# Routing of the first half cut into three pieces and moved behind the last groups, scatters moved behind all inverse roots

## The reference, cut to what matters

```
x = x + attn_a(layernorm(x))      # arccos kernel: 1 - arccos(s)/pi to the power 9, then a product
x = x + ffn(layernorm(x))         # mixture of experts, first time
x = x + attn_b(layernorm(x))      # linear attention: 16 heads of 8, elu feature map
x = x + ffn(layernorm(x))         # mixture of experts, second time

ffn(x):
    logits = x @ gate_w + gate_b
    top_w, top_i = top_k(logits, 2)               # 2 of 8 experts for each token
    gw = softmax(top_w)
    out = sum over the 2 chosen experts e of gw * (gelu(x @ w1[e] + b1[e]) @ w2[e] + b2[e])
    shared = gelu(x @ ws1 + bs1) @ ws2 + bs2
    return out + shared
```

## Time and profile before

| | us |
|---|---|
| median of 3 runs | 698.61 (694.57 to 699.79) |
| profiled execution, its own time | 695.24 |
| its span in the trace | 693.4 |
| busy in the span: DVE / PE / ACT / POOL | 552.1 / 497.8 / 465.5 / 375.5 |

### The profile page before, as it was taken

The page is one execution under the profiler, slowest core; times in us unless marked ns, Lnnn a source line. Parts: engine busy times, 40 slices in busy tenths (PEclk is TensorE's granted clock), DMA queues, the critical chain, the costliest instruction groups (busy, mean ns, idle before and its releaser), DMA issues.

```text
span 693.4 us, 14048 instructions
## 1 busy us (share of the span) xinstructions
PE 497.8 (72%) x3817; PEld 360.3 (52%) x3818; DVE 552.1 (80%) x1229; ACT 465.5 (67%) x937; POOL 375.5 (54%) x382
## 2 busy tenths in 40 slices
PE   1276725655456998999977678757569999999760
PEld 1132305555422446787866466646224469888650
DVE  4989666978668985899989778786679859998991
ACT  1379988998234665989966767845535569999750
POOL 5032201323477776677757722226677737777773
PEclk9999977968558999999999999967689999999996
DMA  8700000000011144444473310001111444545943
GB/s 277 215 8 0 1 0 0 1 1 0 16 47 47 52 115 81 91 98 100 104 194 85 96 35 1 1 9 36 39 48 57 115 80 94 100 101 137 228 112 125
DMA packets 95054, 51.12 MB, mean 74 GB/s; under 512 B 76026, under 2 KB 84180, under 8 KB 94996
## 3 DMA queue, kind: packets, MB, share of 16 engines
q1 hardware_dynamic: 85908, 31.67, 20.5%
q0 software_dynamic: 9088, 18.76, 9.0%
HBM read 16.27 MB, written 23.90 MB: 58 GB/s over the span
## 4 chain that ended last, share of the span: by engine, by line
PE 27%; DVE 21%; issue 17%; ACT 13%; POOL 11%; SPq 8%; DMA 3%; DVEq 0%; POOLq 0%; ACTq 0%
POOL routed_rows L724 8%; SPq L561 5%; PE PC L1107 5%; PE PC L1314 4%; DVE big L1901 2%; DMA RR<-expert_results 2%; DVE RR L1915 2%; ACT SC L834 2%; SPq L568 2%; ACT big L934 2%; PE PA L1125 2%; DVE big L1539 2%; PE PC L1316 2%; PE PA L1296 1%; PE PA L1298 1%
## 5 line engine op out<-in xcount | busy, mean ns | idle before, releaser
L778 POOL DMA_INDIRECT expert_results<-RR,DG x156 | 171.1, 1097 | 73.0 <-issue 45.9
L724 POOL DMA_INDIRECT routed_rows<-big,SLQ x128 | 137.5, 1074 | 56.1 <-issue 45.0
L1314 PE MATMUL PC<-W,big 128*128 x624 | 117.4, 275 | 25.9 <-DVE RR L1915 24.7
L1026 ACT ACTIVATE SC<-PA,B1T,scl 128x256 f32<-128x256 f32 x208 | 100.5, 571 | 21.6 <-PE PA L1298 12.2
L1904 DVE SCALAR_TENSOR_TENSOR big<-SC,scl,big 128x1024 f16<-128x1024 f32 x78 | 100.3, 1286 | 2.8
L1316 PE MATMUL PC<-W,big 128*128 x468 | 86.5, 221 | 0.0
L1314 PEld LDWEIGHTS PC<-W,big 128*128 128x128 f16 x624 | 57.9, 98 | 41.5 <-issue 36.8
L1107 PE MATMUL PC<-QW,big 128*128 128x128 f32 x256 | 42.7, 345 | 42.8 <-DVE big L1539 28.1
L1901 DVE TENSOR_SCALAR big<-SC,scl 128x1024 f16<-128x1024 f32 x78 | 65.1, 835 | 5.8 <-ACT SC L1026 5.8
L671 POOL TENSOR_TENSOR RS<-VA,halfneg 128x4 f32<-128x4 f32 x24 | 28.4, 1185 | 67.9 <-DVE VA L1573 67.8
L1107 PEld LDWEIGHTS PC<-QW,big 128*128 128x128 f32 x256 | 41.2, 257 | 45.0 <-DVE big L1539 29.4
(11 more groups left out here) (284 smaller groups left out, 1268.3 us busy)
## 6 DMA issues: line engine op xcount, KB each, us to landing
RR<-expert_results SPq DMA_DIRECT2D x16, 512.0 KB, 4.2
routed_rows<-pad_zeros SPq DMA_DIRECT2D x23, 128.0 KB
expert_results<-RR,DG POOLq DMA_INDIRECT x156
X<-n_L_attn_a_hidden_states SPq DMA_DIRECT2D x2, 1024.0 KB, 6.5
big<-in_L_ffn_w SPq DMA_DIRECT2D x1, 2048.0 KB, 9.0
routed_rows<-big,SLQ POOLq DMA_INDIRECT x128, 2.4
out_x<-X SPq DMA_DIRECT2D x8, 256.0 KB
big<-routed_rows SPq DMA_TRANSPOSE x78
```

The source lines that it names most:

```text
L724: pool.indirect_dma_start(routed, bass.IndirectOffsetOnAxis(ap=SLQ[:, slot, t, c:c + 1], axis=0), XHL[:, slot, t, c, :].bitcast(I32), None ...
L778: pool.indirect_dma_start(results, bass.IndirectOffsetOnAxis(ap=DG[:, k, r, 0:1], axis=0), YT[:, k, r, :], None).then_inc(result_stored[k] ...
L1026: ins = act.activation(HF[:, k % 3, b * RU:(b + 1) * RU], up_out(k, b), ACT.Gelu, scale=INV1, bias=B1T[:, bass.ds(b1_at + b, 1)])
L1314: last = pe.matmul(both, hh, W2[:, :, at], start=(b == 0), stop=(b == HB - 1))
```

## The change

Three things move; no arithmetic operation is added or taken away.

1. routing is cut into choose, place and gates. For the first half they stand behind the last groups' steps on DVE: in layer 0 choose(0) at the end of step 16, place(0) at the end of step 17, gates(0) and rows(0) behind the add of group 7, then rows(1) and rows(2) at the ends of steps 20 and 22; in layer 1 choose(0) at the end of step 8, place(0) behind the add of group 7 and ahead of its shift, gates(0) and rows(0) behind that shift, rows(1) and rows(2) behind the low part of group 7. rows(3) stands behind the routing of the second half. Places come before gates now.
2. PE's route(0) moves with it: behind the value product of group 7 in layer 0, behind the projection of group 7 in layer 1, there in bank A in place of bank C.
3. On POOL all inverse roots (and in layer 0 all x_scale) come ahead of the first scatter.

The core of the diff (renamed helpers and the unchanged steps are left out):

```diff
              (3, "gate"), (1, "turn_out"))
-LIN_RING = {"kv": "A", "out": "A", "turn_out": "A", "turn_x": "B", "state": "B", "gate_turn": "B",
+LIN_RING = {"kv": "A", "out": "A", "turn_out": "A", "route": "A", "turn_x": "B", "state": "B", "gate_turn": "B",
...
-                if (what, n - lag) == ("project", groups // 2 + 1):
+                t.take(what, n - lag, LIN_RING[what])
+                if (what, n - lag) == ("project", groups - 1):
                     for slot in range(2):
-                        t.take("route", slot, "C")
-                t.take(what, n - lag, LIN_RING[what])
+                        t.take("route", slot, LIN_RING["route"])
     return t.turn
...
             if layer:
-                USES.append(("linear", (3 * per, 3 * per), (3 * per, 3 * per), (3 * per + 1, 3 * per + 1)))
+                USES.append(("linear", (3 * per + 1, 3 * per + 1), (3 * per, 3 * per), (3 * per, 3 * per)))
...
             if half == 0:
-                return PC[slot], c_read[slot], lin_free("route", slot)
+                return PA[slot], a_read[slot], lin_free("route", slot)
...
 
-                    for n in range(NG):
-                        if n >= 2:
+                    for n in range(2, NG + 2):
+                        if n < NG:
                             group_root(n, 2)
-                        if n >= 2:
-                            if n == NG - 1:
-                                scatter(0, 0, 0, range(2))
-                            group_root(n - 2, 3)
-                    scatter(0, 0, 0, range(2, TPG))
-                    group_root(NG - 2, 3)
-                    scatter(1, 0, 1, range(2))
-                    group_root(NG - 1, 3)
-                    scatter(1, 0, 1, range(2, TPG))
-                    for g in range(2, NG):
-                        paced(g)
+                        group_root(n - 2, 3)
                 else:
-                    for g in range(NG - 2):
+                    for g in range(NG):
                         x_scale(g)
                         group_root(g, 1)
-                    x_scale(NG - 2)
-                    scatter(0, 0, 0, range(2))
-                    group_root(NG - 2, 1)
-                    x_scale(NG - 1)
-                    scatter(0, 0, 0, range(2, TPG))
-                    group_root(NG - 1, 1)
-                    scatter(1, 0, 1)
-                    for g in range(2, NG):
-                        paced(g)
+                for g in range(NG):
+                    paced(g)
...
                     straight(NG, [(1, lin_exp_kv), (3, gate_normalise), (2, lin_turn_out), (3, gate_hi),
-                                  (1, lin_exp_q), (0, first_gap), (0, lin_normalise), (0, lin_turn_x),
+                                  (1, lin_exp_q), (NG + 1, first_gap), (0, lin_normalise), (0, lin_turn_x),
...
 
             def value(g):
                 slot = g % 2
-                if g == NG - 1:
-                    route(0)
                 pe.wait_ge(s["p9_ready"], 2 * g + 2)
                 wait(pe, c_read[slot], first_free("value", g))
                 for t in range(TPG):
@@ -1107,6 +1088,8 @@
                         last = pe.matmul(PC[slot][:, t * D:(t + 1) * D], powers, QW[:, b, :],
                                          start=(b == 0), stop=(b == HB - 1))
                 last.then_inc(s["o_ready"], 1)
+                if g == NG - 1:
+                    route(0)
 
             for layer in range(2):
...
 
                 def lin_project(g):
                     k = g % 2
-                    if g == NG // 2 + 1:
-                        route(0)
                     pe.wait_ge(a_read[k], lin_read("turn_out", g))
                     wait(pe, c_read[k], lin_free("project", g))
                     for t in range(TPG):
                         last = pe.matmul(PC[k][:, t * D:(t + 1) * D], OT[k][:, t * P:(t + 1) * P], WOT[:])
                     last.then_inc(s["l_fin"], 1)
+                    if g == NG - 1:
+                        route(0)
 
                 def gate_rows_turn(g):
...
 
                 def gate_logits(g):
                     logits(g, g // 2, g % 2, "")
-                    if g == NG // 2 - 1:
-                        routing(0)
+
+                def first_routing(n):
+
+                    if n == 0:
+                        choose(0)
+                    if n == 1:
+                        place(0)
+                    if n == 2:
+                        gates(0)
                         rows(0)
-                    if NG // 2 <= g < NG - 1:
-                        rows(g - NG // 2 + 1)
+                    if n in (4, 6):
+                        rows(n // 2 - 1)
+
+                def lin_choose(g):
+                    if g == 0:
+                        choose(0)
+
+                def lin_place(g):
+                    if g == 0:
+                        place(0)
+
+                def lin_gates(g):
+                    if g == 0:
+                        gates(0)
+                        rows(0)
+
+                def lin_rows(g):
+                    if g == 0:
+                        rows(1)
+                        rows(2)
 
                 def first_add(g):
...
-                    step(*[dve.tensor_tensor(CB2[:, c, :, :], OH[:, c, :, :], each(GW, c), ALU.mult)
-                           for c in range(2)])
-                    step(dve.tensor_tensor(CB[:, mine, 0:E], CB2[:, 0, :, :], CB2[:, 1, :, :], ALU.add))
-
+                def place(half):
+
+                    step, mine, done = route_step(half, CHOOSE_STEPS), half_tiles(half), 2 * layer + half + 1
                     dve.wait_ge(s["counts_ready"], done)
                     counts, counts_read, counts_free = route_bank(layer, half, 0)
                     places, places_read, places_free = route_bank(layer, half, 1)
...
                            for c in range(2)])
-                    for c in range(2):
-                        ins = dve.tensor_reduce(SLF[:, mine, c], SLT[:, c, :, :], AX.X, ALU.add)
-                    ins.then_inc(s["routed_out_ready"], 1)
-                    assert n[0] == done * ROUTE_STEPS, n[0]
+                    step(*[dve.tensor_reduce(SLF[:, mine, c], SLT[:, c, :, :], AX.X, ALU.add)
+                           for c in range(2)])
+
+                def gates(half):
+
+                    step, mine, done = route_step(half, ROUTE_STEPS - 2), half_tiles(half), 2 * layer + half + 1
+                    dve.wait_ge(s["th_ready"], done)
+                    step(*[dve.tensor_scalar(GW[:, mine, c], TH[:, mine], 0.5 - c, 0.5, ALU.mult, ALU.add)
+                           for c in range(2)])
+                    step(*[dve.tensor_tensor(CB2[:, c, :, :], OH[:, c, :, :],
+                                             GW[:, mine, c:c + 1].to_broadcast([P, HT, E]), ALU.mult)
+                           for c in range(2)])
+                    dve.tensor_tensor(CB[:, mine, 0:E], CB2[:, 0, :, :], CB2[:, 1, :, :],
+                                      ALU.add).then_inc(s["routed_out_ready"], 1)
                     dve.wait_ge(s["routed_out_ready"], done)
-
 
                 def rows(g):
...
@@ -1883,11 +1904,16 @@
 
                 if layer:
                     straight(NG, [(0, lin_combine), (1, lin_elu_k), (4, gate_logits), (0, lin_shift), (3, gate_lo),
-                                  (1, lin_mask), (1, lin_elu_q), (2, lin_add), (1, lin_divide), (2, gate_shift)])
+                                  (NG + 2, lin_rows), (1, lin_mask), (1, lin_elu_q), (2, lin_add),
+                                  (NG + 1, lin_place), (1, lin_divide), (2, gate_shift), (NG, lin_choose),
+                                  (NG + 1, lin_gates)])
                 else:
                     by_units(NG, [(6, first_hi), (0, third, 1), (6, gate_lo), (4, first_shift), (8, gate_logits),
-                                  (1, ninth, 1), (3, first_add)])
-                routing(1)
+                                  (1, ninth, 1), (3, first_add), (2 * NG, first_routing, 1)])
+                choose(1)
+                place(1)
+                gates(1)
+                rows(3)
                 rows(4)
                 gate_parts(0)
```

More of the change, by code:

```diff
@@ L407, in lin_free @@
         def lin_free(what, g):
-            return used(LIN_RING.get(what, "C"), "linear", g % 2) + lin_turn[what, g]
+            return used(LIN_RING[what], "linear", g % 2) + lin_turn[what, g]
         def lin_read(what, g):
@@ L453, in build @@
         s = {n: sem(n) for n in names}
[L454 removed]
+        CHOOSE_STEPS, ROUTE_STEPS = 11, 17
         GATE_STEPS = 5
@@ L1680, in logits, with route_step @@
                         GB[:].unsqueeze(1).to_broadcast([P, TPG, E]), ALU.mult, ALU.add).then_inc(c_read[k], 1)
-                def routing(half):
-                    letter = "ab"[half]
-                    n = [(2 * layer + half) * ROUTE_STEPS]
-                    first, done = half * HT, 2 * layer + half + 1
-                    mine = slice(first, first + HT)
```

(7 more changed lines are left out.)

6 lines of the change are left out of this document (1 added, 5 removed).

## The result

The changed kernel takes 718.57 us (median of 4 runs, 715.19 to 720.51) against 697.06 (694.57 to 699.79): a ratio of 1.032, 95% interval 1.027 to 1.036. It is slower by 21.5. The forecast was slower by about 12; the measured time lies 2.6 above the upper end of the range.

What follows compares the result with a forecast made beforehand. The end of the scatters was taken to set stage 3, in layer 1 narrowly not. Layer 0's 2.9 plus layer 1's 9.7 made 12.6 on 695.24, so 707.8; 1 added gave 709 us, range 700 to 716.

Steps and rivals of the forecast that it cites:

- the 1 to 3 us of slack: Layer 1, stage 3 behind the landing of the last scatter: 3.3 us of slack at unit 7, 1.2 at unit 32.
- DVE's saved stall: Logits of group 7 come about 8 us earlier in layer 0, 6.4 in layer 1; eaten by scatters now behind the last root.
- The starts: First scatter on POOL starts at 188.1 in layer 0 and 485.1 in layer 1.
- 13 intervals at 1.31 and 50 at 1.41: Layer 0's scatters on POOL: 87.5 us in all, last landing at 278.0, 2.9 later than before.
- 12 at 1.30 and 51 at 1.415: Layer 1's scatters on POOL: last landing at 575.2, 12.0 us later; less slack, 9.7.
- The new wait: DVE, rows(4) to rows(7) wait for their slot's scatter; layer 1's stage 2 ends some 4.5 us later, costing nothing more.
- The rival that added 4 us for it (713): PE's lateness of 4.5 in stage 2 is not covered by SP's, so layer 1 costs 14: 713; chance 0.06.
- The rule on the port: While DVE stands in the new wait, scatters run at the quiet pace: layer 1's 12.0 becomes 10.8, the sum 1.2 less.
- rival of the quiet pace: Scatters run at 1.30 throughout in both layers: together 3 us slower, 698 to 700; chance 0.13.
- the gain that arrives (681): The end of the scatters does not bind; DVE's 8.2 in layer 0 and 6.4 in layer 1 pass through; chance 0.06.
- The sum by which the gain was to decide: At SP's wait for all scatters, a pace of about 1.29 gives -4.1 and, less 2.3 of slack, +1 to +2.
- The sign that I named: Would show the forecast right: PE waiting for big<-routed_rows at unit 6 of layer 1.

Runs made afterwards that it cites:

- delay kernel: Kernel before, with five more inverse roots on POOL ahead of the scatters of group 7 in both layers: 710.31 us against 695.88.
- quiet kernel: Changed kernel, with the shared expert's second split cut to 64 of 512 columns from its fifth half group on: 707.36 us against 695.88 for the kernel before.

## Why the prediction was wrong in size

The direction and the path were right, and the pace was wrong, in its size and in what sets it. The landing of the last scatter sets stage 3 of layer 0 one for one (delay kernel), layer 1's has the 1 to 3 us of slack that the earlier trace rows gave at its early units, the eight and twelve scatters that leave the gaps run behind the last root, and DVE's saved stall arrives at the logits (7.5 and 6.6 earlier against 8 and 6.4, less what each layer began with) and is of no use.

- **The starts** were right within 0.7: 188.8 against 188.1, 485.0 against 485.1.
- **The step that failed is the pace, "13 intervals at 1.31 and 50 at 1.41" and "12 at 1.30 and 51 at 1.415".** I took the level of stage 2 as a constant. It is an outcome of how DVE's splits lie against the scatters: 11 intervals of 2.0 in each layer instead of 4, behind DVE's new waits. The 63 intervals took 90.97 instead of 87.5 in layer 0 and 90.26 instead of 87.8 in layer 1, the last flight was 0.7 longer for the same reason, and the landings came 4.8 and about 3.1 behind the forecast. Layer 0 cost 7.1 instead of 2.9, layer 1 12.7 instead of 9.7: 19.8 instead of 12.6.
- **The new wait** I had sized too small and, worse, for the wrong effect. Its end for rows(7) of layer 1 was 532.4 (544.09 less 11.7) instead of 529, PE's unit 0 8.0 late instead of 4.5, and in layer 0 5.7 late where I expected nothing. In all DVE stood 13.2 and 15.1 us. I priced what waits behind DVE, and not that the pile of splits behind each wait then runs in step with the scatters, the very thing that the wait is for: the wait lengthens itself. The rival that added 4 us for it (713) had the right place and too small a price.
- **The rule on the port** that I weighed (the Trainium skill, SBUF — State Buffer, the box on the trap that DVE blocks DMA) says that GpSimd can't write descriptors while VectorE holds the shared pair in a two-port mode. The trace agrees that there is a hold: each of the 36 scatters that began within a 1.28 us split ended 0.82 to 0.85 behind it. In which mode an operation ran, no trace here shows. I used the rule only for the quiet stretches (1.26, even less than the 1.31 of the earlier trace rows), from which 1.2 us less would follow; it speaks as much for the bursts, and these outweighed them.
- **The rival of the quiet pace** (698 to 700) and that of the gain that arrives (681) fell. The quiet kernel reached 1.35 only by cutting DVE's work. The sum by which the gain was to decide, at a pace of 1.29, was off: 63 intervals of 1.29 give a landing at 271.7, 3.4 earlier and not 4.1, and in layer 1 one at 568.7, 5.5 later, which less 2.3 of slack is +3.2 and not +1 to +2. The forecast does not use it.
- **The range.** The upper end took 1.415 throughout as a bound, though the traces behind the earlier trace rows have single intervals of 2.0, the bound of a scatter beside a split. Half of the intervals at 2.0 would have reached past 720. Of the 21.5, 1.7 lie beyond the 19.8: the chance of a late stage 1, which goes with a lower clock (4.6 us in the profile of the change), can cover that, but how much of it each of the four runs had is not known.
- **The sign that I named**, PE waiting for big<-routed_rows at unit 6 of layer 1, did not appear. PE came there 3.8 later, but held by a down-product's bank, which waits for the result that waits for the first tail. Tails of the first six units ahead of SP's wait for all scatters might take that piece off; it wasn't run.

Left open: the division between the layers on a chip where the scatters bind, which rests on the one profile of the change; whether rows that come later would win the pace back there; and why ScalarE stands still on the other chips.

## What to carry to other kernels

Where a queue of small transfers is the path, look at the gaps that its engine has, before moving it: filling them was worth 4 us, emptying them, with the routing moved back, cost about 20. A pace read as a mean over a stage is a property of the overlap of two engines; when the change shifts one of them, bound the sum by the slowest and the quickest single interval. A ring whose slot is freed by that same queue turns its lateness into a pile-up on the engine that fills it, and the pile can slow the queue again.

## What the runs showed of the hardware

- A 128x1024 second split on VectorE (scalar_tensor_tensor, 1.28 us) holds up the issue of an indirect transfer on GpSimd that begins within it, in 36 of 36 cases of the changed kernel: it ends 0.82 to 0.85 behind the split. Begun 0.4 us into the split it takes 1.67 to 1.73 us instead of 0.96, begun 1.1 us into it 1.01 to 1.03. Back to back the two run in step at 1.98 to 2.04 us per scatter. The tensor_scalar of 128x1024 holds it too (0.84 behind its end at 251.16); an addition with one input from a matmul's bank did not (0.96 at 277.87).
- PE's granted clock in stage 1 differs between executions of the same instructions (1.00 or 0.83 in one stretch of 20 us), and with the lower clock the logits of group 3 came 4.6 us later. Between all profiles they differ by up to 6.
- On some chips the same program took 15% longer, with standstills of ScalarE of up to 14 us from the first scatters on, and parts of a change that costs 3% elsewhere cost 0 to 5% there. What else differs between these chips is not in the trace.
